# TensorE's loop over expert turns written out in a two-layer convolution and mixture-of-experts kernel

## What is computed

```
x = x + conv0(ln_c(x));  t = tokens(x);  t = t + moe0(ln_t(t))
x = x + conv1(ln_c(x));  t = tokens(x);  t = t + moe1(ln_t(t))

moe0: top 2 of 8 experts, weights from a softmax over the two logits
      out += cw[:, e] * (silu(xt @ W1[e]) @ W2[e])            W1: 128 x 512, W2: 512 x 128
moe1: top 2 of 8, weights from the softmax, made to sum to 1
      h = silu(x @ w1[e]) * (x @ w3[e]) * combine; out = h @ w2[e]   w1, w3: 128 x 256, w2: 256 x 128
```

## Time and profile before

| | before |
|---|---|
| median of 3 runs | 1513.65 us (1511.8 to 1514.36) |
| the profiled execution's own time | 1519.82 us |
| its span, first to last instruction | 1517.7 us |
| mean granted TensorE clock | 0.852 |
| busy: TensorE matmuls / weight loads | 1118.1 / 880.7 us |
| busy: VectorE / ScalarE / GpSimd | 979.3 / 646.2 / 733.0 us |
| experts of layer 0, from the first to the last load of a block | 416.9 to 740.4 us |
| experts of layer 1, from the first L1044 to the last L1061 | 1198.1 to 1450.6 us |

### The profile page before, as it was taken

The page is one execution under the profiler, slowest core; times in us unless marked ns, Lnnn a source line. Parts: engine busy times, 40 slices in busy tenths (PEclk is TensorE's granted clock), DMA queues, the critical chain, the costliest instruction groups (busy, mean ns, idle before and its releaser), DMA issues. The chain is left out here.

```text
span 1517.7 us, 28287 instructions
## 1 busy us (share of the span) xinstructions
PE 1118.1 (74%) x6195; PEld 880.7 (58%) x6196; DVE 979.3 (65%) x3803; ACT 646.2 (43%) x1295; POOL 733.0 (48%) x703
## 2 busy tenths in 40 slices
PE   0599134431099999999739979889889599999920
PEld 0599133321089999999626546455555478888820
DVE  6766166657056666666466676767775688888844
ACT  2465145532034444444333564555655444444410
POOL 0332177778534444444352265454663765665620
PEclk9999555555599999999959999989989699999965
DMA  9242585411122222222161022021110233333359
GB/s 225 58 113 65 147 259 93 79 49 51 36 67 63 62 62 63 62 64 62 46 180 29 14 57 58 22 64 41 28 31 20 71 98 83 87 85 85 87 137 260
DMA packets 138877, 123.73 MB, mean 82 GB/s; under 512 B 65813, under 2 KB 119310, under 8 KB 137408
## 3 DMA queue, kind: packets, MB, share of 16 engines
q1 hardware_dynamic: 107149, 72.91, 19.7%
q0 software_dynamic: 19968, 39.44, 8.3%
q10 hardware_dynamic: 11667, 10.46, 2.5%
HBM read 72.74 MB, written 51.06 MB: 82 GB/s over the span
## 5 line engine op out<-in xcount | busy, mean ns | idle before, releaser
L645 POOL DMA_INDIRECT routed<-r_xn,r_slot x320 | 339.8, 1062 | 285.2 <-DVEq L634 162.3
L1020 POOL DMA_INDIRECT answers<-e_y,e_dest x152 | 145.8, 959 | 199.0 <-ACT e_y L1140 194.0
L1424 PE MATMUL c_pz<-c_c,down 116*120 116x512 f32 (+1 forms) x392 | 197.1, 619 | 0.0
L1020 POOL DMA_INDIRECT answers<-c_c x152 | 145.9, 960 | 90.8 <-issue 68.6
L1192 DVE COPY e_ht<-e_ps_ht 128x512 f32<-128x512 f32 x152 | 105.2, 692 | 121.6 <-PE e_ps_ht L1061 121.6
L1071 PE MATMUL e_ps_y<-w,e_ht 128*128 x1216 | 160.6, 275 | 0.0
L1398 PE MATMUL c_py<-c_xh,gl 121*116 121x512 f32 (+1 forms) x196 | 123.6, 631 | 33.2 <-DVE c_xl L1527 29.6
L1071 PEld LDWEIGHTS e_ps_y<-w,e_ht 128*128 128x128 f32 x1216 | 147.8, 192 | 0.1
L1537 DVE SCALAR_TENSOR_TENSOR c_c<-c_a 116x1024 f32<-116x1024 f32 (+1 forms) x60 | 76.6, 1277 | 69.1 <-ACT c_a L1482 67.7
L1135 ACT ACTIVATE e_h<-e_ps_h 128x512 f32<-128x512 f32 x154 | 92.0, 598 | 57.8 <-PE e_ps_h L1053 57.8
L1482 ACT ACTIVATE c_a<-c_py 116x512 f32<-116x512 f32 x116 | 68.5, 590 | 105.1 <-PE c_py L1398 102.2
(11 more groups left out here) (206 smaller groups left out, 2915.2 us busy)
## 6 DMA issues: line engine op xcount, KB each, us to landing
answers<-answers SPq DMA_DIRECT2D x32, 480.0 KB, 5.9
e_xg<-routed SPq DMA_DIRECT2D x159, 66.0 KB, 1.8
c_c<-routed SPq DMA_DIRECT2D x159, 66.0 KB, 1.8
c_w<-in_w SPq DMA_DIRECT2D x26, 393.8 KB
routed<-r_xn,r_slot POOLq DMA_INDIRECT x320, 2.4
c_x<-in_xh SPq DMA_DIRECT2D x4, 1170.0 KB, 11.1
w1l<-in_w SPq DMA_DIRECT2D x2, 2048.0 KB, 10.4
out<-x ACTq DMA_DIRECT2D x16, 240.0 KB
```

Source lines behind the costliest of these rows:

```text
L645: ro.nc.gpsimd.indirect_dma_start(ro.xs, bass.IndirectOffsetOnAxis(ap=ro.slot[0:px, q, c:c + 1], axis=0), ro.xn[0:px, q, k, t, :], None).t ...
L1020: ex.nc.gpsimd.indirect_dma_start(ex.ys, bass.IndirectOffsetOnAxis(ap=ex.dest[:, s:s + 1], axis=0), ex.y[:, s, :], None).then_inc(ex.store ...
L1424: ins = nc.tensor.matmul(ps_z[q % 3][0:rows, :], r.down[0:PPX, m * TPX:m * TPX + rows], c[0:PPX, p % R, :], start=p == ROWS * q, stop=p == ...
```

## The change

TensorE runs its turns through `written_out` in place of `steps`, in both layers. `written_out` takes `second_part` and calls it ahead of turn `turn_b`. So TensorE's 18 looped turns a layer are written out: there is no loop counter and no branch, and the values of its waits and the addresses of its table reads are constants. The loads of expert codes, the copy of `held` and the arithmetic on codes stay, as does the order of matmuls and waits. SyncE and GpSimd keep `steps`.

```diff
-    def written_out(self, step):
+    def written_out(self, step, second_part=None):
 
         for it in range(self.STEPS):
+            if second_part is not None and it == self.turn_b:
+                second_part()
             for s in range(self.U):
                 step(it, s, it == 0)
...
-    ex.steps(pe, step, second_part)
+    ex.written_out(step, second_part)
     second_product(BLOCKS - 1, U - 1, weights_of(pe.snap(held, min_val=0, max_val=EXPERTS ** 8 - 1), 0), False)
```

## The result

The changed kernel takes 1505.62 us in the median of 14 runs (1496.08 to 1509.87), the kernel before, run beside it 14 times, 1516.35 (1511.8 to 1520.5). The ratio is **0.9924**, 95% interval 0.9907 to 0.9942, that is 8.8 to 14.1 us less. The forecast was 11.2 us less than the 1513.65 then shown, a ratio of 0.9926. The change is faster, as forecast, and by the amount forecast. One run of a later experiment (e10) took 1716.53 us at a mean granted clock of 0.70 and is left out of that experiment's ratio.

The account below looks back on a forecast made before the run. TensorE's instruction queue was taken to delay layer 1's turns; 17 turns saving 0.31 + 0.23 + 0.10 = 0.64 us each, plus 0.33 for the entered one, gave 11.2 us: 1513.65 to 1502.5, range 1499.5 to 1509.0.

Parts of the forecast that it names:

- Layer 0, 0 us: Layer 0's expert stage: matmuls already hide the jump at 2.14 us a block, so no gain.
- the turn's distance: Layer 1, first-product starts across a turn's end: falls from 2.07 to about 1.53 us.
- first term: Layer 1's jump: the loop's ALU_OP and COMPARE_BRANCH go, 0.31 us a turn.
- second term: Layer 1's turn end: FUSED_REGOPS and ALU_OP that exist only because the turn is a register go, 0.23 us.
- 12.3 us: Layer 1's whole excess over plain blocks in its looped turns, also the gain's high end.
- Rival A: Layer 1's turn end: only the jump goes, the pause stays; gain 5.3 us, 1508.4 us; chance 0.12.
- low end: Layer 1's smallest forecast gain, 8.9 us: 0.51 for 17 turns and 0.20 for the entry.
- Layer 1, step 3: Layer 1's mid-turn load of the second half of expert codes: constant address saves 0.10 us a turn.
- Rival B: Layer 1: no change, as the wait for VectorE is real or VectorE takes over; 1513.7 us; chance 0.06.
- Rival C: Both expert stages: slower by instruction supply, at least 31 packets more, up to 1539.5 us; chance 0.06.

Follow-up runs that it names:

- e10: Changed kernel with the mid-turn expert-code read put in a second held register without bounds arithmetic, and SyncE's and GpSimd's loops written out; ratio 0.9915.
- e2: Changed kernel with TensorE's loop put back in layer 1, layer 0 staying written out; ratio 1.0015.
- e8: Kernel before with two turns in each pass of TensorE's loops, so nine of eighteen jumps a layer go and register values stay; ratio 0.9965.
- e7: Changed kernel with the mid-turn expert-code read put in a second held register, without bounds arithmetic and assert; ratio 0.9929.
- e3: Changed kernel, still written out, but with the turn's number in a register set once a turn, from which waits and addresses are computed; ratio 0.9984.
- e9: Changed kernel with four unused semaphore increments ahead of each turn's first block on TensorE's queue, three instructions more a turn; ratio 0.9975.

## Why the prediction was right

**Layer 0, 0 us.** Right: 308.5 in every profile of the study, looped, written out or with three instructions added. That layer 0 covers the queue is shown; that its cover is the longer second product and the four transposes is argued from the counts, as no run changed them alone.

**Layer 1, the turn's distance.** Forecast 2.07 to 1.53, measured 2.07 to 1.47. The sum 0.31 + 0.23 = 0.54 was nearly the 0.57 to 0.59 measured. **Its first term was too small.** I priced the counter's addition and the branch at 0.31 by the distance where the loop is entered from turn 0, 1.76, as if that place lacked the jump alone. It has an instruction that later turns lack, a MOVE that sets the counter. The loop's entry in the kernel before, TensorE's queue:

```profile
...
L980 PEldq MOVE  x1: 35/35/35, 1224.9 to 1224.9; - x1
...
```

The place is also a poor measure: 1.76 there is one reading, the second profile of the same kernel has 1.89, and e2, whose layer 1 has the same loop, 1.62. The trace of the kernel before had the jump's price in the queue itself, in the turn of the earlier trace rows:

```profile
...
L985 PEldq ALU_OP  x1: 32/32/32, 1325.7 to 1325.7; - x1
L985 PEldq COMPARE_BRANCH  x1: 208/208/208, 1325.8 to 1325.8; - x1
L985 PEldq FUSED_REGOPS  x1: 50/50/50, 1326.1 to 1326.1; - x1
...
...
L1043 PEldq FUSED_REGOPS  x1: 42/42/42, 1326.2 to 1326.2; - x1
...
```

From the first of the loop's three to the instruction behind them are 0.5 us, as e8 measures. Of these 0.49 by the steps above, 0.36 belong to the addition and the branch (I had 0.31) and 0.13 to the FUSED_REGOPS, which I had counted in the second term. That term was 0.23; measured it is these 0.13 and the 0.07 that e8's turn without a jump pays for the register values of its waits and addresses, 0.20. What those values would be worth with the jump left in, no run shows. So the sum is right because both terms are near; but the first rested on one reading of a place that spreads from 1.62 to 1.89, and that this reading was a good one is luck. (Of the 17 turns, one is entered from the first of the two loops without a jump taken; its distance is 2.02.) One slip of arithmetic changes nothing: 11.2 of 12.3 us is 91%, not 89%.

**Rival A** (only the jump goes) was priced too low: with 0.50 a turn for all three instructions of the loop it gives 17 x 0.50 = 8.5 us, not 5.3, and lies close to the forecast's low end of 8.9. That it did not come true can be told by the distance of 1.47, not by the time.

**Layer 1, step 3.** Forecast 0.10 a turn, measured 0.08 in the mean. The addresses' arithmetic is gone; what answers to the earlier trace rows is:

```profile
...
L1035 PEldq TENSOR_LOAD <-table x38: 295/301/324, 430.3 to 1428.0; - x38
L1035 PEldq FUSED_REGOPS  x38: 151/151/165, 430.6 to 1428.4; - x38
L1035 PEldq SEQ_ASSERT  x38: 18/18/28, 430.9 to 1428.6; - x38
...
```

The read of L1035 has one FUSED_REGOPS (38) where there were two (74), and the 0.05 us a turn that remain are the other one with its assert, as e7 shows.

**The total.** Forecast 11.2 us, 11.9 in the stretch and 8.8 to 14.1 in the runs.

**Rival B** (VectorE really bounds it) fell by the start times, as argued: 1314.93 against 1314.87. But VectorE is now the neighbour, 0.06 us away, and its wait for TensorE's transposes shrank to 2.9 us from the 17.4 of the kernel before:

```profile
...
DVE c_c L1192 <- PE c_pz L1061: 17.4, 55, 0.5
...
```

**Rival C** (code supply). The packets rose by 36; 31 and "50 or more" in all were forecast. In the two looped stretches they are, layer 1 then layer 0:

```profile
...
q8 instruction: 15, 0.25, 0.5%
...
```

```profile
...
q8 instruction: 24, 0.39, 0.5%
...
```

Layer 0 had 24 and lost nothing, 308.5 us with 24 packets as with the one of the earlier trace rows. They took 0.005 x 16 x 310 = 25 us in all, 1.0 us each (the forecast had 1.2), so TensorE did not stand still for them. In layer 1 the packets may have left a mark, below.

**The branch.** It takes 0.208 us in e8 as in the kernel before. That is the branch that jumps; the last of each loop, which doesn't, takes 0.076 us. e8's 0.50 for the whole jump is the number to use here.

## What to carry to other kernels

In this kernel a loop's jump costs TensorE only what its instruction queue isn't ahead of its matmuls (0.50 us a turn in layer 1, nothing in layer 0): read the starts of one matmul line over two turns, in each stage by itself, before unrolling. Where matmuls per block are few (10 in layer 1, 16 in layer 0), count queue instructions between the last slow one (a table load) and the matmul that comes late. Read from the trace how far apart they start (here about 0.1 us, 0.27 for a jump); that was about the price of each here once the queue's lead was used up, and the first two of e8 cost 0.07 us together. Moving the load away from the jump gave half the stretch's gain here (6.2 of 11.9 us), with no more code. Where the loop is entered, look for instructions that the loop itself lacks before taking that place as a measurement, and don't rest a term on one reading.

## What was not expected of the hardware

- **The queue's step.** Where the queue has no lead left, TensorE's register instructions of 0.035 and 0.05 us cost 0.27 us for the two of them (e3 beside e8), a semaphore increment of 0.051 us 0.14 (e9).
- **Packets may leave a mark.** In the changed kernel 12 of layer 1's 144 distances are 1.55 to 1.65 us, and 8 of them lie just ahead of a packet of the instruction queue or around it (the packet starts 1.1 to 2.3 us behind the first of the two matmuls); in its second profile 8 of 13. One of them, TensorE in order of time, and the queue from 1336.9 to 1337.9:

```profile
...
1335.16 0.48 PE L1053 MATMUL c_py<-w1h,c_xl 128*128 x1
...
1336.78 0.49 PE L1053 MATMUL c_py<-w1h,c_xl 128*128 x1
```

```profile
...
q8 instruction: 1, 0.02, 7.9%
...
```

  Two ALU_OPs of one line in a row usually start 0.10 us apart. In the first profile of the changed kernel seven such pairs of layer 0 and one of layer 1 are 0.25 us apart, each about 1 us ahead of a packet; in its second profile one is, in layer 1, and in the expert stages of the kernel before none. In layer 0 they cost nothing; in layer 1 it is at most some 0.15 us x 15 packets = 2.3 us, an estimate and not tested by itself.
- **One program's convolution varies.** Its length moved by 2.1 us (kernel before) and 3.4 us (changed kernel) between two executions. The granted clock moved with the length in the one pair shown above, 0.91 and 0.93, but doesn't account for it: over the whole convolution e2 has 451.0 us at 0.91 and the changed kernel's second profile 443.9 at 0.90. Such spread is larger than several effects of this study, which is why they are read from the stretch.
